# A residual addition made by an adding DMA of GpSimd in place of VectorE

## The reference

```python
h = _layernorm(x, axis=-1) * (1 + ca) + sa
x = x + ga * _L0_attn_ref(h, ...)      # x2: the residual after attention
h = _layernorm(x, axis=-1) * (1 + cb) + sb
x = x + gb * _L0_ffn_ref(h, ...)

# _L0_attn_ref, x being h
scores = jnp.einsum('bhld,bhle->bhde', q, k) / jnp.sqrt(dx)
out = jnp.einsum('bhld,bhde->bhle', v, softmax(scores))
out = out.reshape(B, L, H * dx) @ w_fc + b_fc + x
out = (out - mu) * rsqrt(var + EPS) * gamma + beta

# _L0_ffn_ref, x being h; x_prev is x one token earlier
xr = mu_r * x + (1.0 - mu_r) * x_prev
xk = mu_k * x + (1.0 - mu_k) * x_prev
r = sigmoid(einsum('btc,dc->btd', xr, W_r))
k = einsum('btc,dc->btd', xk, W_k)
out = r * einsum('btc,dc->btd', square(relu(k)), W_v)
```

## Time and profile before

| | |
|---|---|
| median of 3 runs | 691.29 us (690.74 to 691.36) |
| the profiled execution | 690.5 us |
| its span, first to last instruction | 688.8 us |
| TensorE matmul busy | 655.9 us, 95% |
| VectorE busy | 573.1 us, 83% |
| ScalarE busy | 456.6 us, 66% |
| GpSimd busy | 277.8 us, 40% |
| mean granted TensorE clock | 0.990 of full |
| DMA of GpSimd (adding), share of 16 engines | 32.6%, 33.03 MB |
| DMA of SyncE, share of 16 engines | 25.2%, 55.97 MB |

### The profile page before, as it was taken

One profiled execution on the slowest core, in us unless ns is written; L12 is line 12 of the kernel. 1 busy time (PEld: TensorE's weight loads), 2 busy tenths in 40 slices (PEclk: granted clock), 3 DMA queues, 4 the chain that ended last, 5 costly groups with the idle time before them and its releaser, 6 DMA issues.

```text
span 688.8 us, 12488 instructions
## 1 busy us (share of the span) xinstructions
PE 655.9 (95%) x3968; PEld 537.5 (78%) x3968; DVE 573.1 (83%) x1328; ACT 456.6 (66%) x983; POOL 277.8 (40%) x499
## 2 busy tenths in 40 slices
PE   8987899999999999999999999999999999999896
PEld 6776786788878887789867887788867898687675
DVE  4994989979788888989799797888889897848973
ACT  1423686676956688656966769567876669666662
POOL 5272631653237242652317432372326533214320
PEclk9989999999999999999999999999999999999998
DMA  8749335574936767284855849267673727548225
GB/s 316 233 153 207 117 107 115 100 178 107 205 87 120 191 120 177 52 184 122 186 95 99 196 99 207 69 141 186 120 161 63 129 75 164 99 81 184 31 31 91
DMA packets 90985, 93.04 MB, mean 135 GB/s; under 512 B 4224, under 2 KB 89000, under 8 KB 90960
## 3 DMA queue, kind: packets, MB, share of 16 engines
q0 software_dynamic: 33264, 33.03, 32.6%
q1 hardware_dynamic: 55344, 55.97, 25.2%
q10 hardware_dynamic: 2352, 3.73, 1.5%
HBM read 42.84 MB, written 33.10 MB: 110 GB/s over the span
## 4 chain that ended last, share of the span: by engine, by line
PE 84%; ACT 6%; DVE 4%; issue 3%; DMA 1%; POOL 1%; ACTq 0%; DVEq 0%; POOLq 0%
PE work L1423 13%; PE gram L1353 11%; PE work L1406 11%; PE work L1237 5%; PE work L1239 4%; PE work L1238 4%; PE gram L1486 4%; PE att L1458 4%; PE tr L1346 4%; PE att L1237 4%; PE att L1238 4%; PE att L1239 4%; PE tr L1390 3%; ACT mx L679 2%; PE att L1477 2%
## 5 line engine op out<-in xcount | busy, mean ns | idle before, releaser
L1423 PE MATMUL work<-mx,w_k_t 128*128 128x512 f32 x244 | 111.8, 595 | 2.4 <-ACT y L689 2.4
L478 POOL TENSOR_TENSOR rs<-ve,neg_half 128x4 f32<-128x4 f32 x32 | 38.9, 1214 | 184.1 <-DVE ve L944 184.1
L1406 PE MATMUL work<-w_r_t,mx 128*128 128x256 f32 x464 | 105.9, 381 | 0.0
L1406 PEld LDWEIGHTS work<-w_r_t,mx 128*128 128x128 f32 x464 | 85.9, 190 | 11.1 <-DVE y L1008 0.3
L717 ACT ACTIVATE z<-x,nm,rs 128x256 f32<-128x256 f32 x128 | 66.3, 592 | 39.5 <-POOL nm L480 39.5
L1353 PE MATMUL gram<-z 128*128 128x256 f32 (+1 forms) x512 | 89.1, 327 | 0.0
L1423 PEld LDWEIGHTS work<-mx,w_k_t 128*128 128x128 f32 x244 | 45.9, 190 | 50.8 <-issue 40.6
L1353 PEld LDWEIGHTS gram<-z 128*128 128x128 f32 x512 | 79.8, 191 | 6.5
L1237 PE MATMUL work<-wvf_lo,k_hi 128*128 128x256 f32 x248 | 74.0, 298 | 10.1 <-issue 10.1
L1237 PE MATMUL att<-m_lo,z_hi 128*128 128x256 f32 x248 | 74.3, 300 | 4.5 <-DVE t_buf L923 2.5
L652 ACT ACTIVATE sq<-att 128x256 f32<-128x256 f32 x124 | 45.6, 380 | 40.6 <-PE att L1239 40.6
(11 more groups left out here) (186 smaller groups left out, 1595.2 us busy)
## 6 DMA issues: line engine op xcount, KB each, us to landing
x_in<-in_L_attn_x_dram SPq DMA_DIRECT2D x32, 512.0 KB, 4.9
x<-rows SPq DMA_DIRECT2D x32, 512.0 KB, 3.5
x<-in_L_attn_x_dram POOLq DMA_DIRECT2D x32, 512.0 KB, 8.4
out_dram<-x SPq DMA_DIRECT2D x31, 512.0 KB, 5.5
out_dram<-y POOLq DMA_DIRECT2D x29, 512.0 KB, 6.0
rows<-row_scratch SPq DMA_DIRECT2D x16, 128.0 KB, 5.0
rows<-row_scratch SPq DMA_DIRECT2D x8, 256.0 KB, 3.7
wqkv_sb<-in_L_attn_w_qkv_dram ACTq DMA_DIRECT2D x1, 1536.0 KB, 10.0
```

The lines of the kernel that those rows point to most:

```text
L1406: ins = mm(r_banks(alone)[q][:, (t % 2) * D:(t % 2 + 1) * D], mixed(j)[0][:, ch, tile], w_r_t[:, ch], start=(ch == 0), stop=(ch == KD - 1))
L1423: ins = mm(k_banks(alone)[dh][:], w_k_t[:, ch, rows_dh], mixed(j)[1][:, ch], start=(ch == 0), stop=(ch == KD - 1))
```

## The change

`make_x2` is split. `make_t` writes t_buf as before; the addition is made by GpSimd's `add_t`, an adding DMA from t_buf to x2, both in SBUF, 512 KB in rows of 4 KB. A product of two small constants stands in front of it on GpSimd. `stats_2` and the next writer of t_buf (`make_t` of the next piece, `take_wvf`) wait for that DMA (x2_added). `store_x2` waits for the statistics, which read the finished x2. In the last row VectorE makes the addition as before. VectorE's list is put in another order around this, GpSimd's list gets the four `add_t`, and on ScalarE `take_r(b, 1)` and `scale_k(b, 2)` change places; TensorE's and SyncE's orders stay.

```diff
--- before.py
+++ after.py
@@ -141,6 +141,7 @@
         rs_o = sb("rs_o", [P, 2, NT])
         t_buf = sb("t_buf", [P, NT, D])
         x2 = sb("x2", [P, CH, NT, D])
+        t_seen = sb("t_seen", [P, CH, NT])
         st_2 = sb("st_2", [P, 2, NT, 6])
         ag_2 = sb("ag_2", [P, 2, NT, 2])
         neg_2 = sb("neg_2", [P, 2, NT])
@@ -266,6 +267,7 @@
         rs_o_ready = sem("rs_o_ready")
         t_done = sem("t_done")
         x2_ready = sem("x2_ready")
+        x2_added = [sem(f"x2_added{j}") for j in range(CH)]
         st_2_done = sem("st_2_done")
         ag_2_done = sem("ag_2_done")
         rs_2_done = sem("rs_2_done")
@@ -351,7 +353,7 @@
 
             def store_x2(b, j):
 
-                sp.wait_ge(x2_ready, CH * b + j + 1)
+                sp.wait_ge(st_2_done, CH * b + j + 1)
                 sp.dma_start(out_v[b, j], x2[:, j]).then_inc(x2_stored[j], 16)
 
             def row_x2(b, j):
@@ -486,6 +488,13 @@
                 pool.wait_ge(ve_o_done, i + 1)
                 nc.gpsimd.tensor_tensor(rs_o[:, s], ve_o[:, s], neg_half[:], ALU.pow).then_inc(rs_o_ready, 1)
 
+            def add_t(b, j):
+
+                pool.wait_ge(t_done, CH * b + j + 1)
+                pool.wait_ge(x2_filled[j], 16 * (b + 1))
+                nc.gpsimd.tensor_tensor(t_seen[:, j], half[:], half[:], ALU.mult)
+                nc.gpsimd.dma_start(x2[:, j], t_buf[:], accum_op=ALU.add).then_inc(x2_added[j], 16)
+
             def fill_x2(b, j):
 
                 pool.wait_ge(x2_rowed[j], 16 * (b + 1))
@@ -520,25 +529,27 @@
                 rstd_o(b, 0)
                 if not first:
                     add_y(b - 1, 2)
+                add_t(b, 0)
+                if first:
+                    rstd_a(n, 2)
+                else:
                     fill_x2(b, 2)
                 rstd_2(b, 0)
+                rstd_o(b, 1)
+                add_t(b, 1)
                 if first:
-
-                    rstd_o(b, 1)
-                    rstd_a(n, 2)
-                    rstd_2(b, 1)
-                    rstd_o(b, 2)
                     rstd_a(n, 3)
-                else:
-                    rstd_o(b, 1)
-                    rstd_2(b, 1)
-                    rstd_o(b, 2)
+                rstd_o(b, 2)
+                rstd_2(b, 1)
+                if not first:
                     add_y(b - 1, 3)
                     fill_x2(b, 3)
+                add_t(b, 2)
                 rstd_2(b, 2)
                 rstd_o(b, 3)
                 add_y(b, 0)
                 fill_x2(n, 0)
+                add_t(b, 3)
                 rstd_2(b, 3)
                 if far:
                     rstd_a(n + 1, 0)
@@ -752,8 +763,8 @@
                 copy_gram_low(n)
                 copy_h2(b, 2)
                 scale_r(b, 2)
+                take_r(b, 1)
                 scale_k(b, 2)
-                take_r(b, 1)
                 take_k(b, 1)
                 copy_gq(n)
                 make_z2(b, 3)
@@ -912,10 +923,15 @@
                                                   ag_a[:, j, 7, t:t + 1], ALU.subtract, ALU.mult)
                 ins.then_inc(z_ready, 1)
 
-            def make_x2(b, j, mixes=0, alone=False):
+            def make_t(b, j, mixes=0, alone=False):
 
                 i, s = CH * b + j, j % 2
-                wait_past(dve, x2_ready, i)
+                if j == 0:
+                    wait_past(dve, x2_added[CH - 1], 16 * b)
+                elif alone:
+                    dve.wait_ge(x2_ready, j)
+                else:
+                    dve.wait_ge(x2_added[j - 1], 16 * (b + 1))
                 if mixes:
                     dve.wait_ge(xk_mixed, CH * b + mixes)
                 dve.wait_ge(rs_o_ready, i + 1)
@@ -923,13 +939,21 @@
                     ins = nc.vector.scalar_tensor_tensor(t_buf[:, t], att_banks(j, alone)[t // 2][:, (t % 2) * D:(t % 2 + 1) * D],
                                                          rs_o[:, s, t:t + 1], g_row[:], ALU.mult, ALU.mult)
                 ins.then_inc(t_done, 1)
+
+            def make_x2(b, j, mixes=0):
+
+                i = CH * b + j
+                make_t(b, j, mixes=mixes, alone=(j > 0))
                 dve.wait_ge(t_done, i + 1)
                 dve.wait_ge(x2_filled[j], 16 * (b + 1))
                 nc.vector.tensor_tensor(x2[:, j], t_buf[:], x2[:, j], ALU.add).then_inc(x2_ready, 1)
 
-            def stats_2(b, j):
+            def stats_2(b, j, alone=False):
                 i, s = CH * b + j, j % 2
-                dve.wait_ge(x2_ready, i + 1)
+                if alone:
+                    dve.wait_ge(x2_ready, j + 1)
+                else:
+                    dve.wait_ge(x2_added[j], 16 * (b + 1))
                 for t in range(NT):
                     ins = nc.vector.bn_stats(st_2[:, s, t], x2[:, j, t])
                 ins.then_inc(st_2_done, 1)
@@ -972,7 +996,7 @@
                 dve.wait_ge(r_done, 2 * i - 2)
                 dve.wait_ge(k_done, 2 * i - 2)
                 dve.wait_ge(xk_mixed, i)
-                dve.wait_ge(x2_ready, CH * b + made)
+                dve.wait_ge(x2_ready, made)
                 dve.wait_ge(h2_ready, 2 * i + 2)
                 prev = h2t[:, :, j * CT:(j + 1) * CT]
                 nc.vector.tensor_tensor(dif, h2t[:, :, 1 + j * CT:1 + (j + 1) * CT], prev, ALU.subtract).then_inc(dif_done, 1)
@@ -1021,7 +1045,7 @@
             def take_wvf(b, alone=False):
 
                 if not alone:
-                    dve.wait_ge(x2_ready, CH * b + 2)
+                    dve.wait_ge(x2_added[1], 16 * (b + 1))
                 wvf = w_v_t[:] if alone else t_buf[:, 0:KD]
                 dve.wait_ge(gb_loaded, 16 * (b + 1))
                 nc.vector.tensor_tensor(wvf, w_v_t[:], rows[:, 2].unsqueeze(1).to_broadcast([P, KD, D]),
@@ -1103,39 +1127,38 @@
                 take_g(b)
                 prep_now(n)
                 low_z(n, 0)
-                make_x2(b, 0)
-                stats_2(b, 0)
+                make_t(b, 0)
                 if first:
                     stats_a(n, 2)
                     stats_a(n, 3)
-                    low_z(n, 1)
-                    make_x2(b, 1)
-                    stats_2(b, 1)
-                    make_z(n, 2)
+                    stats_2(b, 0)
                 else:
                     make_z(n, 2)
                     low_k(b - 1, 3)
+                    stats_2(b, 0)
                     prep_qk(n)
-                    low_z(n, 1)
-                    make_x2(b, 1)
-                    stats_2(b, 1)
+                low_z(n, 1)
+                make_t(b, 1)
+                if first:
+                    make_z(n, 2)
                 mix_r(b, 0)
                 mix_k(b, 0)
+                stats_2(b, 1)
                 low_z(n, 2)
                 if first:
                     prep_qk(n)
                 else:
                     gate_o(b - 1, 3)
                 take_wvf(b)
-                make_x2(b, 2)
+                make_t(b, 2)
+                make_z(n, 3)
+                low_k(b, 0)
                 stats_2(b, 2)
-                low_k(b, 0)
-                make_z(n, 3)
                 mix_r(b, 1)
                 low_z(n, 3)
                 gate_o(b, 0)
                 mix_k(b, 1)
-                make_x2(b, 3)
+                make_t(b, 3)
                 mix_r(b, 2)
                 mix_k(b, 2)
                 low_k(b, 1)
@@ -1150,31 +1173,32 @@
                     stats_a(n + 1, 1)
                     make_z(n + 1, 0)
                     stats_a(n + 1, 2)
-                    make_z(n + 1, 1)
                 low_k(b, 2)
                 make_m(n)
                 mix_r(b, 3)
                 mix_k(b, 3)
                 if far:
+                    make_z(n + 1, 1)
+                if far:
                     stats_a(n + 1, 3)
                 gate_o(b, 2)
 
             def last_row(b):
                 take_g(b)
                 make_x2(b, 0)
-                stats_2(b, 0)
-                make_x2(b, 1, alone=True)
-                stats_2(b, 1)
+                stats_2(b, 0, alone=True)
...
```

10 lines of the change are left out of this document (6 added, 4 removed).

## The result

The changed kernel takes **794.7 us** (median of 4 runs, 793.4 to 796.2) against 691.3 us of the kernel before in the same comparison: 1.150 times as long, 95% interval 1.147 to 1.1525. The prediction was 794. Its profiled execution took 796.2 us with a span of 794.4, so the span grew by 105.6 us.

The account below looks back on a forecast made before the run. TensorE was taken to bound the kernel. Rows 1 to 5 lose 14.8 - 1.3 + 1.7 = 15.2 us each, row 6 16.2, row 0 10.8: 103 in all, on 690.5 gives 793.5, forecast 794 us, range 740 to 822.

Parts of the forecast that it names:

- T1: Moment t_buf is ready for piece 1 (pieces are 512 tokens, numbered 0 to 3): A + 28.5, where it was A + 23.1.
- T2: Moment t_buf is ready for piece 2: A + 43.0, 7.7 us late.
- The gain of the order: TensorE's waits at row end and for ScalarE's y shrink: 1.3 us a row, 0.3 in row 6.
- The landing of a DMA alone: Adding DMA from t_buf to x2 lands 5.9 us after issue, 6.2 from t when the queue is empty.
- The queue: GpSimd's adding DMAs queue, 2.8 us each; piece 2's DMA stands behind add_y(b - 1, 3) and fill_x2(b, 3).
- Piece 0: DMA behind add_y(b - 1, 2) completes x2 at A + 17.7; negated mean 3.9 us later, at A + 21.5.
- Piece 1: x2 complete at T1 + 6.2, after the two mixes end, so VectorE stands; stats_2 takes 2.2, the rest to t 6.1.
- ScalarE's order: make_z2 of pieces 0 and 2 stands ahead of other ScalarE steps, so waiting for the mean holds those back.
- The clock: TensorE's granted clock falls behind the stall before turn_z2(b, 2), costing 1.7 us a row.
- rival of the short landing: New DMA lands in 3.5 us like the plain on-chip copy: 55 us in all, 746 us; chance 0.27.
- rival with the clock at both stalls: Load behind a store lands after 9.6, clock falls at both stalls of a row: 26 us more, 820 us; chance 0.14 (over 808).
- Faster: DMA hidden, only the order's gain of 8 us left: 683 us; needs piece 2's mean at most 0.5 us late; chance 0.02.

Follow-up runs that it names:

- s1: Kernel before with two moves only, make_z(n + 1, 1) behind mix_k(b, 3) and take_r(b, 1) ahead of scale_k(b, 2), no adding DMA: 683.3 us.
- p1: Changed kernel with x2 padded by 8 floats behind each tile of 256, so no run of bytes there exceeds 1 KB: 815.6 us.
- a1: Changed kernel with ScalarE's z2 of pieces 0 and 2 moved behind the steps that don't need it: 768.7 us.
- q1: Changed kernel with GpSimd issuing the adding DMA of piece 2 ahead of the store of y and the load of x: 767.7 us.
- q2: Changed kernel with GpSimd issuing the adding DMAs of pieces 2 and 0 ahead of the store and load that stood before them: 755.4 us.
- g1: Changed kernel with VectorE's prep_qk(n) moved from behind the statistics of piece 0 into the wait before those of piece 2: 783.8 us.
- o1: Changed kernel without add_t: VectorE makes the addition right behind t, every list stays in the changed order: 747.5 us.
- h3: Adding DMA for piece 3 alone, VectorE's and ScalarE's lists otherwise the kernel before with two moves, GpSimd's order the changed kernel's: 688.5 us.

## Why the prediction was right, point by point

The time was right to 0.7 us, and in the middle rows for the reasons given; some sizes behind it were off and offset each other. With the landing of 4.6 us that piece 1 shows and all else left alone, the sum would have been 1.3 us less in each of six rows, by my estimate some 786. So the range was reasoned, and the last 8 us of agreement are luck. A is the start of attention (b, 0), 339.4.

| step | predicted | measured |
|---|---|---|
| T0 | A + 10.1 | A + 10.7 |
| x2 of piece 0 | A + 17.7 | A + 18.0 |
| negated mean of piece 0 | A + 21.5 | A + 23.1 |
| T1 | A + 28.5 | A + 30.0 |
| x2 of piece 1 | A + 34.7 | A + 34.8 |
| T2 | A + 43.0 | A + 42.9 |
| load ahead in the queue lands | A + 49.4 | A + 49.8 |
| x2 of piece 2 | A + 52.2 | A + 53.0 |
| mean of piece 2 | A + 56.1 | A + 56.6 |
| turn_z2(b, 2) | A + 61.4 | A + 62.1 |
| row, rows 1 to 5 | 95.2 us | 95.5 us |

- **What bounds the kernel:** right. VectorE lost 36 us of work and TensorE's waits decided the time.
- **The gain of the order:** right; s1 measured it alone at 8.0 us, the number of the prediction.
- **The landing of a DMA alone:** too long by 1.3 us at piece 1. I took 5.9 from GpSimd's adding loads and stores; in piece 1 of rows 1 to 6 it was 4.6 every time, between my two bounds (3.5 and 6.0). p1 shows the layout to be part of it: 5.4 with 1 KB runs; no run shows what makes the rest. What runs beside it seems to count too. In those six places SyncE moves next to nothing; in row 0 it moves 0.87 and 0.72 MB beside the DMAs of pieces 1 and 2, which landed after 6.1 and 6.8, and in a1 1.05 MB beside that of piece 1 (6.8 or 7.1). No run changed SyncE's transfers alone, so their part in it is read from these places and not shown; and the DMA of piece 0 in row 0 took 6.1 with 0.01 MB beside it, which stays unexplained. The Trainium skill, "DMA: Bandwidth & Descriptors", section "Anatomy of one DMA — SWDGE (gpsimd) path", gives 2.0 us plus the bytes over 436 GB/s, by which I estimate 3.2 us for 512 KB; the traces don't agree (4.6 at the least).
- **The queue:** right. Piece 2's DMA landed 9.8 after its issue (9 predicted) and 3.2 behind the load ahead of it (2.8); q1 and q2 show its price.
- **Piece 0:** the DMA landed 0.3 late (its own landing took 6.6 with the store ahead of it; the load that I had put in its place took 8.4 behind a store, and the DMA went out later, at 350.74, once t was seen). The mean was 1.6 late: 0.3 from that, and 1.2 because the two small instructions of GpSimd took 2.67 us and not the 1.49 that is in my 3.9. `prep_qk` used to run behind them, now it starts with them: I had asked which queues a step is moved past, not which instruction it comes to lie beside. The Trainium skill, "GPSIMD Engine Reference", section "Specifications", says that GpSimd shares its SBUF interface with VectorE and contends with VectorE's instructions of two SBUF inputs; by it rs would be slow beside `prep_qk`, and the trace agrees (1.99 us against 1.03 in g1).
- **Piece 1:** here the two errors offset. T1 came 1.5 us late, and the shorter landing gave it back: x2 was there 4.8 after T1, not 6.2, and T1 to T2 took 12.9 us where I had 14.5. It could have given back no more, since the two mixes ended at the same moment (VectorE waited for nothing at 374.20).
- **ScalarE's order:** right, and only half of the story. a1 showed it as a link (26 us), with the mean itself as the next limit: TensorE then stood 2.7 and 5.1 us a row before turn_z2 of pieces 0 and 2, for z2.
- **The waits named ahead:** before bn_stats of pieces 0, 1 and 2 some 1.5, 1 to 2 and 5 us were named, and 1.93, none and 5.36 are there; TensorE's some 4 and 7 us were 5.16 and 7.59; ScalarE's two waits for the mean are there.
- **The clock:** it fell twice a row, to 0.57 and 0.56 over 5 us, not once. The second fall costs about 2.0 us, by my estimate half of the 3.9 us from the end of the wait (401.46) to the rise of the clock near 405.4; 1.7 was predicted. The first makes TensorE's work longer too (82.66 us of busy time in the row against 78.31) but costs nothing that I can find: the mixes that it made later ended at 374.20, as x2 landed, T2 was not late, and behind T2 TensorE waits before `turn_z2(b, 2)` whatever its clock was. That a stall must be long for the clock to fall, as my rival of the short landing took for row 0, isn't so either: in o1 it fell behind 2.14 us. So the rival with the clock at both stalls had the falls right and their price wrong.
- **The sum:** rows 1 to 5 grew by 77.4 us (76 predicted), row 6 by 14.6 (16.2), row 0 by 10.9 (10.8), between the starts of attention (b, 0). Of the other 2.8 of the 105.6, 2.5 lie ahead of row 0, whose attention began at 60.64 and had begun at 58.15, and 0.3 in the last row. The former scatters: row 0 began between 57.99 and 60.64 in the fourteen profiles of this case. In row 0 the DMA landed after 6.1 to 6.8, near my 5.9, and the clock fell at both stalls (5.29 and 6.59 us).
- **The rivals:** the short landing (3.5) was nearer in piece 1, at 4.6, but the mixes held that piece; the other two lay behind the queue. Faster needed the two waits of ScalarE not to exist, and they do.
- **What I said too simply:** "VectorE stands between t and the statistics" was costed as the DMA's length. o1 shows that the covering work alone holds the mean of piece 0 by 4 us, and that the order costs 56 us without any DMA. The prediction had the 2.8 us of this for piece 2 in its rival "faster" and left piece 0's 4 out. With the DMA in place the cost is hidden in it, so the sum didn't suffer.

Left open: the extra 0.3 us of TensorE's busy time in a row of h3, what lengthens a landing with nothing ahead of it (6.1 us for the very first), and how much of p1's 21 us is the adding DMA's own.

## What to carry to other kernels

An addition made by a DMA doesn't cost the 1.2 us of the engine that is relieved but a way of 5 to 10 us, here from t to the statistics (7.3, 4.8, 10.2 and 10.2 for the four pieces of the middle row: GpSimd's notice, the issue, the queue, the landing, the steps moved in as cover), so compare that way with how long each consumer could have waited, and take it only where there is room, which among the four places here was the last. Where the relieved engine doesn't bound the kernel, even that place gains nothing. When steps are moved to cover a wait, run the move without the wait: here it cost 56 us by itself, and two small moves that came with it were worth 8 alone. And when a change reorders several lists, take each back separately: GpSimd's new order, which looked like a side matter, held t of a piece back by 3.0 us in the first row of h3.

## What the runs showed of the hardware

- An adding DMA on chip, 512 KB from SBUF to SBUF in runs of 4 KB, landed 4.6 us after its issue with nothing ahead of it and next to nothing beside it (six of six in one place); with 1 KB runs at one end 5.4. Its issue took GpSimd 0.93 and 1.31 us.
- With nothing ahead of it but SyncE's transfers beside it, it landed after 6.1 us (0.87 MB beside it, row 0) and 6.8 us (1.05 MB, a1). Once, in row 0, it took 6.1 with 0.01 MB beside it.
- Behind a store and a load of GpSimd it landed after 9.8 us, 3.2 behind the load; issued ahead of them, after 5.1 or 5.2 in q2.
- GpSimd's rs (128x4) took 1.99 us beside VectorE's `prep_qk` and 1.03 without it; nm took 0.68 and 0.20.
- TensorE's granted clock (full is 2.4 GHz) was 0.50, the lower of its two levels, in the later part of waits of 5.2 and 7.6 us and for some 4 us behind them: 0.57 and 0.56 over 5 us, and 1.00 in the next 5. It also fell behind waits of 3.1 and 2.1 us (o1), and eight transposes took 1.97 us at the lower level and 1.04 at the upper.
